# Two fused transformer layers on one core: context rounding moved to GpSimd, gate-and-up chunks over three PSUM banks

## The reference

```python
x = x + _L0_xattn_ref(_layernorm(x), ctx_2048)           # stage a: tokens and context rounded to e4m3 by blocks, product
x = x + _L0_ffn_ref(_layernorm(x), gate_w, up_w, down_w, gate_s, up_s, down_s)   # stage b
x = x + _L1_xattn_ref(_layernorm(x), ctx_2048, mask)     # stage c: attention over the context
x = x + _L1_ffn_ref(_layernorm(x), w_gate, w_up, w_down) # stage d: Hadamard, ternary weights

def quant_dequant_weight_128x128(w):      # the context, in blocks of 128x128
    amax = jnp.max(jnp.abs(wb), axis=(2, 4), keepdims=True)
    q = (wb * (FP8_MAX / safe)).astype(jnp.float8_e4m3fn)
    return q.astype(jnp.float32) * (safe / FP8_MAX)
# stage a: y[m, n] = sum_k xq[m, k] * wq[n, k]
# stage b: g = (x @ gate_w.T) * gate_s; u = (x @ up_w.T) * up_s     (1408 columns each)
#          out = ((silu(g) * u) @ down_w.T) * down_s
```

## Time and profile before

| | |
|---|---|
| time, median of 3 runs | 705.13 us (704.87 to 706.69) |
| the profiled execution's own time | 709.98 us |
| its span | 708.0 us |
| PE busy | 642.6 us (91%) |
| DVE busy | 584.5 us (83%) |
| ACT busy | 470.0 us (66%) |
| POOL busy | 363.6 us (51%) |
| the eight groups of stages a and b on PE | about 39.8 to 315 us of the span |

### The profile page before, as it was taken

How to read it: one execution, slowest core, us unless ns; L and a number is a source line. 1 busy time by engine, 2 the same in 40 slices (tenths; PEclk the granted TensorE clock), 3 DMA queues, 4 the chain that set the end, 5 groups by cost and what they waited for, 6 DMA issues and landing times.

```text
span 708.0 us, 12360 instructions
## 1 busy us (share of the span) xinstructions
PE 642.6 (91%) x4055; PEld 376.8 (53%) x4086; DVE 584.5 (83%) x1331; ACT 470.0 (66%) x965; POOL 363.6 (51%) x277
## 2 busy tenths in 40 slices
PE   1689799999999999997979999899999999999986
PEld 0266466757675666763434444354555555555543
DVE  6889899999999888357759894679899998999775
ACT  3747467766776655377758761466888788887834
POOL 2022131323222314057646751019999999999970
PEclk9999999999999999999999999999999999999999
DMA  8981223333331332708999971144468765667411
GB/s 208 237 287 23 78 79 103 95 102 93 87 103 33 104 76 68 250 11 199 261 166 343 222 192 38 31 88 92 91 120 133 133 136 104 132 125 140 108 46 45
DMA packets 173130, 88.21 MB, mean 125 GB/s; under 512 B 150546, under 2 KB 152594, under 8 KB 172052
## 3 DMA queue, kind: packets, MB, share of 16 engines
q1 hardware_dynamic: 167188, 71.94, 44.8%
q10 hardware_dynamic: 3408, 11.27, 5.0%
q0 software_dynamic: 2480, 4.33, 3.5%
HBM read 51.20 MB, written 4.19 MB: 78 GB/s over the span
## 4 chain that ended last, share of the span: by engine, by line
PE 55%; DVE 23%; issue 7%; ACT 7%; DMA 6%; POOL 2%; SPq 0%; DVEq 0%; ACTq 0%
PE ps L1892 13%; PE ps L1739 7%; PE ps L1964 7%; PE ps L1834 7%; PE ps L1816 6%; DMA arena<-arena 5%; PE ps L1754 4%; PE ps L1872 3%; PE ps L1932 3%; DVE X L1148 3%; DVE arena L1239 2%; PE ps L1691 2%; DVE arena L1081 1%; PE ps L1665 1%; PE ps L1941 1%
## 5 line engine op out<-in xcount | busy, mean ns | idle before, releaser
L1739 PE MATMUL ps<-arena 128*128 128x256 f16 x1408 | 160.1, 273 | 10.3 <-DVE arena L1239 6.7
L1739 PEld LDWEIGHTS ps<-arena 128*128 128x128 f16 x1408 | 135.6, 98 | 36.0 <-DVE arena L1239 10.4
L488 POOL TENSOR_TENSOR arena<-arena 128x256 f16<-128x256 f32 x88 | 57.7, 675 | 181.6 <-ACT arena L663 181.2
L1892 PE MATMUL ps<-arena 128*128 128x512 bf16 x486 | 115.4, 379 | 6.8 <-ACT arena L877 2.9
L560 POOL TENSOR_TENSOR arena<-arena 128x1024 f32<-128x1024 f32 x44 | 104.0, 2363 | 21.8 <-DVE arena L1536 17.3
L561 POOL TENSOR_TENSOR arena<-arena 128x1024 f32<-128x1024 f32 x44 | 103.9, 2362 | 0.0
L1754 PE MATMUL ps<-arena 128*128 128x512 f16 x352 | 80.1, 384 | 3.6 <-POOL arena L488 3.5
L1892 PEld LDWEIGHTS ps<-arena 128*128 128x128 bf16 x512 | 49.1, 98 | 60.0 <-DVE arena L1528 3.5
L656 ACT ACTIVATE arena<-ps,gs 128x256 f32<-128x256 f32 x88 | 40.7, 466 | 51.8 <-PE ps L1739 51.7
L1834 PE MATMUL ps<-arena 128*128 128x512 f16 x256 | 59.4, 387 | 4.7 <-issue 3.6
L1964 PE MATMUL ps<-arena 128*128 128x512 bf16 x251 | 59.1, 379 | 2.3 <-ACT arena L955 1.8
(11 more groups left out here) (167 smaller groups left out, 1200.8 us busy)
## 6 DMA issues: line engine op xcount, KB each, us to landing
arena<-in_ctx_t SPq DMA_DIRECT2D x7, 1024.0 KB, 6.1
arena<-in_wg_t SPq DMA_DIRECT2D x16, 256.0 KB, 3.8
arena<-in_wu_t SPq DMA_DIRECT2D x16, 256.0 KB, 4.4
arena<-in_wd_t SPq DMA_DIRECT2D x16, 256.0 KB, 5.0
arena<-in_ctx_n SPq DMA_DIRECT2D x4, 1024.0 KB, 10.8
arena<-in_wu_t ACTq DMA_DIRECT2D x4, 1024.0 KB, 5.6
arena<-in_wd_t ACTq DMA_DIRECT2D x4, 1024.0 KB, 6.0
out_x<-X SPq DMA_DIRECT2D x16, 256.0 KB, 2.3
```

What stands on the lines that cost most here:

```text
L488: nc.gpsimd.tensor_tensor(hl[:, c, at:at + 2 * P], b_h[n % 4], hh[:, c, at:at + 2 * P], ALU.subtract).then_inc(b_hl_r, 1)
L1739: last = M(bank(n % 2)[:, 2 * P * i:2 * P * i + 2 * P], W[:, b, c * P:c * P + P], part[:, b, at:at + 2 * P], start=(b == 0 and part is xhT ...
L1892: last = M(bank(2 * (n % 2) + i), d_qT[u][:, b, :], W[:, b, D * n:D * n + D], start=(b == 0), stop=(b == KD - 1))
```

## The change

Three PSUM banks (0, 1 and 6, in turn by c) serve the gate-and-up chunks instead of two, with three silu buffers. Bank 6 is shared with the even tiles' down product, so chunk 2 of a group waits until DVE has read that product, and the small context products move from bank 6 to bank 7. DVE's `context_low` (16 instructions) and, for batches 1 to 3, `context_rounding` (24 instructions) move to POOL, into POOL's written order. In group 0 `context_high` of batch 0 moves ahead of the group on ACT, and some context steps of batch 1 stand later.

(`ahead` in the diff is true in groups 2 and 4.)

```diff
+        def gu_bank(c):
+            return (0, 1, 6)[c % 3]
 @block.gpsimd
+            def context_low(e, b):
+                pool.wait_ge(c_hi_r, KD * e + b + 1)
+                nc.gpsimd.tensor_tensor(context_part(e, b, 1), wdq[:, e % 2, b, :], context_part(e, b, 0), ALU.subtract).then_inc(c_lo_r, 1)
+            def context_rounding(e, b):
+                pool.wait_ge(c_grid, 8 * e + 2 * b + 2)
+                nc.gpsimd.tensor_tensor(w, w, grid, ALU.add).then_inc(c_round, 1)
+                pool.wait_ge(c_round, rounds_by(e, b) - 1)
+                nc.gpsimd.tensor_tensor(w, w, grid, ALU.subtract).then_inc(c_round, 1)
...
             root("a", 1, 1)
+            context_low(0, 0)
             root("a", 2, 0)
             root("b", 0, 0)
+            context_low(0, 1)
+            context_low(0, 2)
             root("b", 1, 1)
+            context_low(0, 3)
...
@@ b_group(g) on GpSimd
+                if g == 1:
+                    context_rounding(1, 2)
+                    context_rounding(1, 3)
+                if ahead:
+                    context_rounding(e, 0)
                 h_low(g, 0)
...
                 h_low(g, 1)
+                if g == 1:
+                    context_low(1, 2)
                 h_low(g, 2)
                 h_low(g, 3)
+                if g == 1:
+                    context_low(1, 3)
+                if ahead:
+                    context_rounding(e, 1)
                 h_low(g, 4)
                 h_low(g, 5)
+                if g == 0:
+                    context_rounding(1, 0)
+                if ahead:
+                    context_rounding(e, 2)
...
                 h_low(g, 10)
+                if g == 0:
+                    context_low(1, 0)
+                    context_rounding(1, 1)
                 if n0 + 2 < NT:
                     root("a", n0 + 2, 0)
...
@@ b_group(g) on ScalarE, behind b_high(g, 10)
+                if g == 0:
+                    context_scaled(1, 3)
+                    context_back(1, 0)
+                    context_high(1, 0)
                 if more:
                     b_normal(n1)
...
@@ gate_up_b on TensorE
-                wait(pe, b_h_r, n - 1)
+                wait(pe, b_h_r, n - 1 if c < 2 else n - 2)
+                if c == 2:
+                    if g == 0:
+                        pe.wait_ge(ds_r, 1)
+                    else:
+                        pe.wait_ge(b_scaled, 2 * g - 1)
```

More of the change, by code:

```diff
@@ L114, in fused_blocks @@
         b_xh, b_xl = ([cut(kb + u, 256, fp16) for u in range(2)] for kb in (68, 70))
[L115 removed]
+        b_sil = [cut(72 + u, 256) for u in range(3)]
         b_h = [cut(76 + u, 256) for u in range(4)]
@@ L490, in b_group @@
             def b_group(g):
-                more, n0, n1 = g + 1 < PAIRS, 2 * g + 2, 2 * g + 3
+                more, odd, e, n0, n1 = g + 1 < PAIRS, g % 2 == 1, (g + 2) // 2, 2 * g + 2, 2 * g + 3
+                ahead = not odd and 0 < g and e < B
+                if g == 1:
[3 more added lines that the diff above has]
+                    context_rounding(e, 0)
                 h_low(g, 0)
@@ L503, in b_group @@
                 h_low(g, 7)
+                if ahead:
+                    context_low(e, 0)
                 h_low(g, 8)
@@ L671, in b_group @@
                 sums = (0, 0, 3, 5, 8, 10, 13, 16, 16)
+                ahead = not odd and e < B and g
                 b_silu(g, 0)
-                if g == 0:
-                    context_high(0, 0)
                 if g == 1:
@@ L723, in b_group @@
                 b_high(g, 6)
-                if not odd and e < B and g:
+                if ahead:
                     context_back(e, 0)
@@ L728, in b_group @@
                 b_silu(g, 8)
+                if g == 0:
+                    b_silu(g, 9)
                 if more:
                     b_normal(n0)
-                if not odd and e < B and g:
+                if ahead:
                     context_back(e, 1)
                     context_high(e, 1)
[L734 to L737, removed]
+                if g:
+                    b_silu(g, 9)
                 if not more:
@@ L1264, in b_group @@
                     a_grids(n0)
-                if not odd and e < B and g:
-                    context_rounding(e, 0)
+                if ahead:
                     context_grid(e, 1)
-                if g == 1:
-                    context_rounding(1, 3)
                 if not more:
@@ L1286, in b_group @@
                     mask_rows()
-                if g == 0:
-                    context_low(0, 1)
-                if not odd and e < B and g:
+                if ahead:
                     context_grid(e, 2)
[L1291 to L1297, removed]
                 if more:
                     a_normal(n1)
-                if not odd and e < B and g:
-                    context_rounding(e, 1)
                 if g == 0:
@@ L1324, in b_group @@
                 b_hidden(g, 7)
-                if not odd and e < B and g:
+                if ahead:
                     context_grid(e, 3)
-                if g == 0:
-                    context_rounding(1, 0)
                 if odd and following < B:
@@ L1338, in b_group @@
                     b_center(n0)
+                    a_parts(n1, 1)
+                if g == 0:
+                    b_hidden(g, 9)
+                if more:
+                    b_low(n0)
                 if g == 0:
                     context_grid(1, 1)
-                if more:
-                    a_parts(n1, 1)
-                if not odd and e < B and g:
-                    context_low(e, 0)
-                if more:
-                    b_low(n0)
-                if not odd and e < B and g:
-                    context_rounding(e, 2)
-                if g == 0:
-                    context_grid(1, 2)
-                b_hidden(g, 9)
+                if g:
+                    b_hidden(g, 9)
                 if more:
@@ L1359, in b_group @@
                 if g == 0:
-                    context_rounding(1, 1)
                     dve.wait_ge(ds_r, 1)
-                if not odd and e < B and g:
-                    context_low(e, 1)
+                    context_grid(1, 2)
                 if more:
```

82 lines of the change are left out of this document (37 added, 45 removed).

## The result

The changed kernel takes 725.61 us (median of 4 runs, 724.15 to 726.76) against 705.0 us (703.83 to 706.69) of the kernel before on the same chip: ratio 1.028, 95% interval 1.0256 to 1.0304. It is slower, as forecast, but by 20.6 us and not by 4.4; the time lies above the range.

A forecast was written before the change was run, and what follows sets the result against it. DVE was taken to hold groups 0, 1, 2 and 4 above PE's floor. Group 1's start +1.4, group 1 +3.2, clock +0.7, groups 2 and 4 -1.0, group 3 +0.1 gave +4.4 us: 709.5 us, range 702.5 to 713.5.

The forecast's parts named there:

- Start of group 0, end of group 0: Group 0 starts 0.9 us later; POOL's chain to tile 4's root makes group 1 start 1.4 us later, at 82.3.
- Group 1 without the clock: In group 1 tile 4's product waits for low(1, 3) on POOL until S+17.1; the group takes 3.2 us longer.
- the first failed step: In groups 2 and 4, exclusion takes 5.5 of 7.8 us relief; 0.5 us won each, bounds 2.2 won and 2.0 lost.
- the second failed step: In group 1 PE's clock falls to the lower level after an idle stretch: 0.7 us lost, bounds 0 and 1.7.
- Three banks and group 3: Banks remove PE's waits for hidden, 0 to 0.6 us a group, no own term; group 3 0 within 0.4.
- The last 2 us: Whole kernel: the profiled execution's 4.85 us above the median of runs is carried over, 714.4 becoming 709.5 us.
- the full exclusion: Rival: each moved POOL instruction blocks DVE for its full length; groups 2 and 4 lose 2.0 us each, 714.5 us; chance 0.13.
- Relief in full: Rival: DVE's relief of 28.6 us lets groups 1, 2 and 4 reach PE's floor, 7.4 us won, 697.7 us; chance 0.15.

The follow-up runs named there:

- mended order: Changed kernel with tile 4's root ahead of batch 1's first POOL work, two low parts ahead of group 1's h_low 1, low(0, 3) behind tile 3's root; ratio 1.0122.
- The probe: Three-bank kernel, DVE's work unchanged, plus 11 idle POOL additions that nobody waits for in each of groups 2 and 4; ratio 1.0123 to the kernel before.

## Why the prediction was wrong in size

The sum can be closed. In the profiled executions group 7 starts 18.8 us later than before (308.36 against 289.53): 7.8 us are the clock (changed kernel against the one with idle matmuls) and 11.0 are not. The forecast had 0.7 and 3.7.

- **Start of group 0, end of group 0: right.** Group 1 starts at 82.19, forecast 82.3; DVE idles 5.85 us on the root, forecast some 6. DVE's normalisation ahead of group 0 took 1.17 us (0.55 before), forecast 1.4. The mended order confirms the cause: that chain, not DVE, held group 0, and its relief there was worth 3.7 us (3.1 against three banks alone). Part of that relief is batch 0's: its low parts stood on DVE inside group 0 before, from 43.2 us on, and on POOL they are done ahead of the group but for one.
- **Group 1 without the clock: right.** +3.9 us against +3.2; the product's last part came at S+17.3 against S+17.1. The order is the cause (37.05 us when mended).
- **Groups 2 and 4: the first failed step**, "Then 2.3 us are left of DVE's relief [...] so I count only 0.5 us won in each of the two groups". Without the clock they lost 3.0 us each: 7.0 us off in all, and 1.0 beyond the worse bound. The size of the exclusion was right. Groups 2 and 3 together (windows cut work between neighbours differently before and after) lost 12 instructions of DVE, about 0.66 us each from start to start, 7.9 us; DVE's busy time went from 66.2 only to 65.4 us with the clock held up, so 7.1 us, 0.6 for each moved instruction (0.5 forecast). What failed is the subtraction of one from the other. DVE's idle time in the two groups rose from 3.4 to 7.2 us: the stretched instructions are the grids, normalisations and scales on the chain that PE waits for, and the relief came at places where DVE then waited, in group 2 twice and 2.0 us in all for ACT's silu (line 704), where with three banks alone it did not. The probe shows the first half alone: exclusion with no relief is paid in full, 3.9 of 3.9 us. For the second half the check is a sum: 35.2 us with three banks, plus some 5.3 us of stretch that I count in group 2, makes 40.5; 38.66 were measured, so about 1.8 us of the relief of 7 reached the end of the group. Which waits took the rest was read from the traces and not tried apart; that it came with the four pairs and not with the three low parts is shown by the run with the pairs back on DVE.
- **The clock: the second failed step**, "I take half of it, 0.7 us; bounds 0 and 1.7". It was 7.8 us, shown by the idle matmuls (9.4 by the ratios). I had priced one fall, in group 1, and its full price was right: 1.66 us in groups 3 and 5, 1.1 in groups 2 and 4. There were six stretches, because the exclusion and the order lengthened PE's waits: 2.18 us ahead of the product of tile 7 (1.02 with three banks alone, at full clock), 2.02 at the start of group 3 (0.57 with three banks alone). These waits were followed by falls that cost 1.1 and 1.7 us more. Not every such wait was: in groups 0 to 5 of all the traces a wait of 1.99 to 2.38 us was followed by a fall ten times and seven times not, four of the seven in the kernel with the mended order (2.07, 2.19, 2.01 and 1.99 us). No run here tells what decides it, so the number of falls was not to be had from the waits alone.
- **Three banks and group 3: right.** The banks alone win 0.5 us in groups 2 and 4 (0 to 0.6 forecast) and nothing in the total; with the moved work, at full clock, they win 1.2 us in group 2 (39.87 with two banks, 38.63 in the mended order); group 3 is as long as before without the clock.
- **The last 2 us.** "It stood 4.85 us above the median of the runs [...] and I carry the difference over" took off 3.7 us too much: the profiled execution of the changed kernel stood only 1.15 us above its own median. Behind the groups that execution was 1.9 us quicker than the one before, which no run here explains.

Of the rivals, the full exclusion (groups 2 and 4 lose 2.0 us each, 714.5 us) was nearest, with the right sign and place; but a moved instruction held DVE for some 0.6 us and not for its whole 1.2, and DVE still had 7.2 us of waits in groups 2 and 3 where that rival left no room for any. Relief in full was refuted by the kernel with the mended order: with the order put right and group 0 paying, it is still 1.2% slower.

The Trainium skill (SBUF — State Buffer, Who interferes with whom) adds to the rule named above that a DVE instruction with two SBUF inputs contends with a GpSimd instruction that reads SBUF and not with one that only writes it, while DVE's two-port modes contend with either. The runs agree: line 1110 1.52 us beside additions and 0.69 at most beside memsets, line 1105 stretched by both. That line 1105 runs in a two-port mode no trace here shows.

## What to carry to other kernels

Work moved from VectorE to GpSimd is not gone from VectorE: in groups 2 and 3 some 0.6 us came back for each moved 0.66 us. Price both on the chain, not in sums: the stretch falls on whatever runs beside it, and an instruction that stood where VectorE waits anyway frees nothing when it leaves. Where work is moved, it belongs behind, not ahead of, the small root that everybody waits for. And count TensorE's waits that grow: each that was followed by a fall of the clock cost 1.1 to 1.7 us more than itself, even in groups 3 and 5, which had lost only one low part each.

## What the runs showed of the hardware

- POOL's 128x512 float32 addition and subtraction from two different inputs to float32 take 1.27 to 1.28 us in the median (lines 483, 485), its subtraction to float16 1.16 (line 478), an addition of one tile to itself 1.04, a memset 0.52.
- Small operations are shut out like large ones: DVE's 128x4 operation of line 1162 takes 0.20 us alone (at 120.78) and 0.98 when it starts inside POOL's low part (at 160.10, line 478).
- DVE's reads of PSUM go on beside POOL: in the kernel with the idle additions line 1177 (PSUM and one SBUF tile) ran beside one of them ten times and was never more than 0.02 us longer than at its shortest.
- The third bank gathers PE's waits: before, group 2 had waits of 0.32 and 0.54 us at chunks; with three banks it has one of 1.02 us ahead of the product. With the moved work there were 1.03 and 1.61 us with two banks and one of 2.18 with three.
